# Another order of stages on four engines of a whole-program kernel

## What is computed

```python
# layer 0
mem = memory @ W_mem.T
attn = softmax(x @ mem.T / sqrt(D)); context = attn @ mem
gate = sigmoid(concat([x, context]) @ W_gate.T + b_gate)
x = rmsnorm(x + gate * context, norm_w)
# layers 1 and 3; vm: token and its successor are both of type 1
n = rmsnorm(x, ln_in); q, k, v = split(where(vm, n @ v_qkv, n @ l_qkv))      # 16 heads of 16
ctx = causal_attention(rotary(q), rotary(k), v)
x = x + where(vm, ctx @ v_dense, ctx @ l_dense)
x = x + cross_attention(rmsnorm(x, ln_cross) @ cq_w, context_rows @ ckv_w) @ cdense_w
m = rmsnorm(x, ln_post)
x = x + where(vm, mlp(m, v_weights), mlp(m, l_weights))      # down(silu(gate(m)) * up(m)), 688 wide
# layer 2
x = x + tanh(g1) * masked_attention(layernorm(x) @ Wq, media @ Wkv) @ Wo      # 16 heads of 64
x = x + tanh(g2) * gelu(layernorm(x) @ W1) @ W2
```

## Time and profile before

| | |
|---|---|
| median of 3 runs | 1376.25 us (1374.81 to 1379.65) |
| the profiled execution | 1375.08 us, its span 1372.8 us |
| mean granted TensorE clock of the span | 0.978 of full speed |
| TensorE busy | 1306.5 us (95%), 10931 matmuls |
| vector engine, ScalarE, GpSimd busy | 761.5, 467.8 and 457.3 us (55%, 34%, 33%) |
| DMA traffic | 27.28 MB, mean 20 GB/s |

### The profile page before, as it was taken

One profiled execution on the slowest core, in us unless ns is written; L12 is line 12 of the kernel. 1 busy time (PEld: TensorE's weight loads), 2 busy tenths in 40 slices (PEclk: granted clock), 3 DMA queues, 4 the chain that ended last, 5 costly groups with the idle time before them and its releaser, 6 DMA issues.

```text
span 1372.8 us, 25897 instructions
## 1 busy us (share of the span) xinstructions
PE 1306.5 (95%) x10931; PEld 1055.0 (77%) x10931; DVE 761.5 (55%) x1361; ACT 467.8 (34%) x779; POOL 457.3 (33%) x559
## 2 busy tenths in 40 slices
PE   7898899999999999999999999998899999999988
PEld 5775677877877778888888888876578777787766
DVE  2645666656656756444344553345566657576553
ACT  3333234324233133243344434433442332423321
POOL 1232444435434433311111211224444254344332
PEclk9787899999999999999999999999999999999999
DMA  9001000000001001120000000011000000000000
GB/s 321 12 2 61 2 2 2 1 2 2 1 2 47 1 5 43 44 72 1 0 1 1 1 0 1 1 42 42 1 2 1 2 17 1 2 17 2 1 16 16
DMA packets 19900, 27.28 MB, mean 20 GB/s; under 512 B 3432, under 2 KB 15552, under 8 KB 19520
## 3 DMA queue, kind: packets, MB, share of 16 engines
q1 hardware_dynamic: 19008, 24.20, 5.3%
q10 hardware_dynamic: 768, 1.26, 0.3%
HBM read 23.35 MB, written 2.10 MB: 19 GB/s over the span
## 4 chain that ended last, share of the span: by engine, by line
PE 81%; DVE 6%; POOL 5%; ACT 4%; issue 3%; ACTq 0%; DVEq 0%; POOLq 0%
PE bank L956 5%; PE bank L1100 5%; PE bank L1246 5%; PE bank L1211 4%; PE row_banks L1360 4%; PE bank L1216 4%; PE bank L1420 4%; PE bank L1463 4%; PE bank L1456 4%; PE row_banks L1083 4%; PE row_banks L1050 3%; PE bank L1235 3%; PE bank L949 2%; PE bank L1018 2%; PE bank L1221 2%
## 5 line engine op out<-in xcount | busy, mean ns | idle before, releaser
L1816 DVE TENSOR_REDUCE room<-row_banks 128x4 f32<-128x512 f32 (+1 forms) x128 | 116.5, 952 | 24.8 <-PE row_banks L1055 24.4
L806 POOL TENSOR_SCALAR_AFFINE_SELECT room<-room 128x1024 f32<-128x1024 f32 x64 | 70.4, 1103 | 167.6 <-ACT room L1574 167.6
L1574 ACT ACTIVATE room<-row_banks 128x1536 f32<-128x1536 f32 x64 | 93.0, 1452 | 81.7 <-PE row_banks L1083 81.6
L1246 PE MATMUL bank<-room,down_w 128*128 128x256 f32 x384 | 94.0, 384 | 0.5 <-DVE room L1916 0.5
L1606 ACT ACTIVATE room<-bank 128x256 f32<-128x256 f32 x96 | 36.4, 383 | 134.9 <-PE bank L1216 125.6
L1246 PEld LDWEIGHTS bank<-room,down_w 128*128 128x128 f32 x384 | 69.6, 190 | 12.3 <-issue 3.3
L1830 DVE RECIPROCAL room<-bank 128x256 f32<-128x256 f32 x32 | 56.1, 1754 | 39.3 <-PE bank L1100 39.2
L768 POOL TENSOR_TENSOR room<-room 128x256 f32<-128x256 f32 x32 | 24.7, 772 | 157.7 <-ACT room L1586 157.7
L1586 ACT ACTIVATE room<-x_all 128x512 f32<-128x512 f32 x32 | 20.2, 630 | 151.9 <-DVE x_all L1885 93.8
L1083 PE MATMUL row_banks<-room 32*128 32x256 f32 (+1 forms) x1024 | 62.8, 360 | 7.8 <-ACT room L1574 4.0
L1899 DVE SCALAR_TENSOR_TENSOR room<-room,bank 128x256 f32<-128x256 f32 x96 | 39.9, 416 | 53.3 <-ACT room L1606 53.2
(11 more groups left out here) (243 smaller groups left out, 3043.4 us busy)
## 6 DMA issues: line engine op xcount, KB each, us to landing
out_x<-wq SPq DMA_DIRECT2D x8, 256.0 KB, 2.3
qkv<-in_L_xattn_v_qkv SPq DMA_DIRECT2D x2, 768.0 KB, 5.9
qkv<-in_L_xattn_l_qkv SPq DMA_DIRECT2D x2, 768.0 KB, 8.9
gate_w<-in_L_xattn_v_gate SPq DMA_DIRECT2D x2, 640.0 KB, 8.6
gate_w<-in_L_xattn_l_gate SPq DMA_DIRECT2D x2, 640.0 KB, 7.5
up_w<-in_L_xattn_v_up SPq DMA_DIRECT2D x2, 640.0 KB, 6.0
...
```

What stands on the lines that cost most here:

```text
L806: pool.affine_select(out=diagonal, in_=diagonal, compare_op=ALU.is_ge, fill=0.0, base=0, pattern=[[0, 8], [1, P]], channel_multiplier=-1)\
L1246: return pe.matmul(ff_bank[0][:, t * S:(t + 1) * S], down_w[:, f, t * P:(t + 1) * P], hid[:, i, :], start=(i == t == 0), stop=(i == UPS - ...
L1574: act.activation(probs[w % 2], row_banks[:, :, 0:3 * P], ACT.Exp).then_inc(*ATT_ACT.does(e, f"exp{w}"))
L1816: last = dve.tensor_reduce(dst, row_banks[:, :, P * i:P + S * i], X, ALU.max, negate=True)
```

## The change

Only the table `ORDER` is written anew. It has the same stages for each engine, each once. Of TensorE's 1150 stages 496 stand at another place, of ScalarE's 613 345, of the vector engine's 723 358, of GpSimd's 401 239, of SyncE's 8 none; none is more than 13 places away from where it was. The table takes one line more, so each line number after it is one higher than before. The diff of the table, cut to a line of TensorE's old and new order and one of the vector engine's:

```diff
...
-        f_context.2 f_context.0 f_gate.2 f_gate.1 f_turn.3 f_context.3 f_sum.2 f_gate.0 f_spread.2 f_gate.3 f_sum.1
...
+        f_context.1 f_turn.3 f_gate.2 f_context.3 f_gate.1 f_gate.0 f_gate.3 f_sum.1 f_sum.2 f_sum.0 f_mem.0.3
...
-        f_gated.1 f_mean.2 p_seen.0 f_gated.0 f_mean.1 f_gated.3 f_mean.0 f_y.1 f_y.0 f_mean.3 f_y.2 f_shift.4
...
+        f_shift.0 p_one_hot.0 f_shift.2 f_shift.1 f_sums.0 p_trig_out.0 f_sums.2 f_sums.1 f_shift.3 f_sums.3 p_seen.0
...
```

More of the change, by code:

```diff
@@ L191 @@
-        first_scores.3.1 crs_spread.1.1 k.4 v.4 memory.2 first_scores.3.2 dense.2 up.1.0 up.1.1 crs_sum.2.0
-        first_scores.3.3 crs_spread.2.0 up.1.2 cross_q.2 n0_sum.5 up.1.3 n0_spread.5 cross_first.2 up.1.4 turn_max.3
-        up.1.5 second_scores.3.0 late_up.1.0 second_scores.3.1 values.3.0 cross_turn_max.2 second_scores.3.2
-        late_up.1.2 values.3.1 second_scores.3.3 late_up.1.1 cross_second.2 values.3.2 values.3.3 cross_values.2
-        down.1.0 late_down.1.0 late_down.1.1 late_down.1.2 cross_project.2 down.1.1 down.1.2 down.1.3 crs_sum.2.1
@@ L196 @@
-        down.1.4 down.1.5 crs_spread.2.1 first_scores.4.0 q.5 k.5 first_scores.4.1 memory.3 v.5 dense.3
+        first_scores.3.0 down.0.0 down.0.1 cross_project.1 down.0.2 down.0.3 down.0.4 crs_sum.1.1 first_scores.3.1
+        crs_spread.1.1 down.0.5 q.4 k.4 memory.2 first_scores.3.2 dense.2 v.4 up.1.1 up.1.0 crs_sum.2.0
+        first_scores.3.3 crs_spread.2.0 up.1.2 n0_sum.5 cross_q.2 up.1.3 n0_spread.5 cross_first.2 up.1.4 turn_max.3
+        up.1.5 second_scores.3.0 cross_turn_max.2 late_up.1.0 second_scores.3.1 values.3.0 late_up.1.2
@@ L202 @@
[L202 to L205 removed]
+        crs_spread.3.1 down.2.5 q.6 k.6 v.6 memory.4 first_scores.5.2 dense.4 up.3.0 up.3.1 crs_sum.4.0
@@ new lines @@
+        n0_spread.13 up.9.3 cross_first.10 up.9.4 turn_max.11 up.9.5 second_scores.11.0 late_up.9.0 second_scores.11.1
+        values.11.0 late_up.9.2 second_scores.11.2 cross_turn_max.10 values.11.1 second_scores.11.3 late_up.9.1
+        cross_second.10 values.11.2 values.11.3 cross_values.10 down.9.0 down.9.1 down.9.2 cross_project.10
+        late_down.9.0 down.9.3 down.9.4 down.9.5 crs_sum.10.1 late_down.9.1 late_down.9.2 crs_spread.10.1 turn_out.8
+        turn_out.9 first_scores.12.0 q.13 memory.11 first_scores.12.1 k.13 v.13 dense.11 first_scores.12.2 up.10.0
@@ L288 @@
[L288 to L291 removed]
+        cross_values.11 first_scores.13.0 down.10.0 down.10.1 cross_project.11 q.14 crs_sum.11.1 down.10.2 down.10.3
@@ new lines @@
+        crs_spread.11.1 down.10.4 down.10.5 v.14 memory.12 first_scores.13.1 k.14 up.11.0 dense.12 first_scores.13.2
+        n0_sum.15 up.11.1 crs_sum.12.0 up.11.2 crs_spread.12.0 n0_spread.15 first_scores.13.3 cross_q.12 up.11.3
+        cross_first.12 turn_max.13 up.11.4 up.11.5 second_scores.13.0 late_up.11.0 second_scores.13.1
+        cross_turn_max.12 values.13.0 second_scores.13.2 values.13.1 second_scores.13.3 late_up.11.1 cross_second.12
+        values.13.2 values.13.3 cross_values.12 down.11.0 down.11.1 late_up.11.2 down.11.2 down.11.3 down.11.4
```

561 lines of the change are left out of this document (276 added, 285 removed).

## The result

| | before | the new order |
|---|---|---|
| median, first comparison | 1377.53 us (4 runs, 1374.81 to 1379.65) | 1361.42 us (4 runs, 1354.47 to 1363.33) |
| ratio, 95% interval | | 0.9875 [0.9835, 0.9915] |
| the same kernel again, 5 runs | 1379.26 us (15 runs) | 1361.43 us, ratio 0.9873 [0.9854, 0.9893] |
| profiled execution, its span, clock | 1375.08, 1372.8 us, 0.978 | 1361.10, 1359.1 us, 0.979 |

The new order is 16 to 18 us faster, where 5 were forecast and 1363 was the lower end of the range. In the two profiles the difference is 14.0 us. Before's profiled execution was one of its quicker ones: of 62 runs of it beside the experiments nearly all took 1375 to 1381 us.

A forecast was written before the change was run, and what follows sets the result against it. TensorE's own work was taken as the bound (81% of the chain), so only waits and low clock could be won. Terms -3 - 0.5 + 0 - 0.5 - 0.7 + 0.5 + 0 = -4.2, with clock -5: 1371.2 us, range 1363 to 1380.

The forecast's parts named there:

- Fusion: Layer 0, 20 to 57 us: p_seen moves into the vector engine's 9.02 us hole, TensorE waits shrink; -3 us, bounds -2 and -4.5.
- what is late next is the first pow, which takes 3.02 us: Layer 0: GpSimd's first pow would end at 49.8 us, leaving TensorE a wait of 2.4 us ahead of f_spread.1.
- The three steady stretches: 200 to 560, 560 to 880 and 1020 to 1300 us: no wait worth filling, some stages late; +0.5 us, bounds 0 and +3.
- Hand-over: Layer 2 to 3, 880 to 900 us: n0_sum.9 and n0_spread.9 move into gaps of the chain; -0.5 us, bounds 0 and -0.9.
- Cross attention: 950 to 1000 us: v.11, values.9.3 and crs_sum.8.0 fill TensorE's waits; -0.7 us, bounds -1.5 and +1.5.
- 60 to 100 us: f_sum.7 moves behind f_spread.5, whose wait of 0.73 us shrinks as its mean comes earlier; -0.5 us, bounds 0 and -0.7.
- 100 to 200: 100 to 200 us, first expert: TensorE's order and its waits along the score chain stay; 0 us, bounds -0.6 and +0.6.
- The fall at 95.2 us: Low clock behind the 0.73 us wait, where 12 matmuls take 4.44 instead of 2.84 us; half of 1.6 us counted, 0.8.
- signs of being wrong: Include: steady stretches lack 3 us more or clock under 0.99; low time from 40 to 200 us over 10 off 48; f_gated.2 late.
- The clock: Whole kernel: with fewer waits some low clock goes, 0.8 us, taking the forecast from -4.2 to -5 us.
- The rival of more gain: Layer 0: the clock's fall at 54.2 us doesn't come, so 7.7 us more go; 1360 to 1366 us, chance 0.14.
- The slower rival: Steady stretches: new 1 us waits, each with a clock fall, cost 4.3 us apiece; 1380 to 1384 us, chance 0.18.

The follow-up runs named there:

- e2: The kernel before with only p_seen moved ahead of f_gated.2 on the vector engine; median 1375.58 us, ratio 0.9982.
- e5: The new kernel with p_seen moved back from ahead of f_gated.2 to behind f_mean.2, beside the pows; median 1368.13 us, ratio 0.9929 to the kernel before.
- e7: The kernel before with one GpSimd pair swapped, crs_rstd.3.0 ahead of turn_q.5; run once, 1380.44 us, only its timeline used.
- e11: The kernel before with the new order only from 888 to 1020 us of the old times; median 1376.14 us, ratio 0.9977.
- e10: The new kernel with the old order put back from 955 to 1020 us; median 1361.26 us, ratio 0.9873 to the kernel before.
- e4: The kernel before with the new order only from 880 to 1020 us of the old times; median 1380.31 us, ratio 1.0014.

## Why the prediction was wrong

**Sign and main mechanism were right**, and the size was wrong by a factor of three, outside the range. By its own steps:

- *Fusion, -3 us.* Measured -6.5 to -6.8 (6.0 from the start of the execution, where this one loaded 0.7 us late). p_seen went into the hole as said. The step that failed is "what is late next is the first pow, which takes 3.02 us": it was priced as a property of the first pow, and carried into the new order at full price, while it was p_seen that made it slow (e2, e5). That is 2.0 of the 3.6 us (a wait of 0.43 for one of 2.4). The rest is ahead of the gates: f_gate.2 starts at 29.64 us instead of 30.96, 14.1 instead of 16.1 us after x_turn.1, which I had set equal. The bound of -4.5 was too tight for the same reason.
- *The three steady stretches, +0.5 us with bounds 0 and +3.* Measured -4.7 up to 803 us and -0.8 from 1018 to 1306. This is the largest miss in sign. Two things failed: "there is no wait worth filling" was read from a busy share, which shows less than a wait costs (0.70 us for 0.48 shown), and the bounds left out any gain, though 8.5 us of idle time stood in the rows. The two table loads of ScalarE cost nothing that I can see, and no wait of TensorE there is longer than 0.61 us.
- *Hand-over, -0.5.* Measured -1.7: 0.2 to 0.4 by the moved work, no more than chance, and the rest by 3.4 us less at the low clock behind the wait, which I hadn't priced there and which isn't the order's (e7, e11).
- *Cross attention, -0.7.* The waits shrank by more than I said, the time didn't (+1.2 in the profile). Against e10, which has the old order there, it is -0.8, about as forecast. What hid it is the clock, 10 us more of it low than in before's profile.
- *60 to 100 us, -0.5 and 0.8 for the clock.* Measured -1.3 in all, which looks right, but by luck: the second profile of the same kernel has +0.4, with 14 us of low clock instead of 10. *100 to 200, 0:* -0.9. The fall at 95.2 us, which I had half going, is gone in both profiles of the new kernel, and v.0 runs at the high clock: that is 3.4 us less of low clock behind the start of v.0, and near the 0.8 that I had counted for it. From 40 to 200 us TensorE is low for 37 us in the new profile and 41 in the second, instead of 48; a difference over 10 was one of my signs of being wrong.
- *The clock.* Its part is 3 us smaller in the new kernel, where I had 0.8. The rival of more gain rested on the fall at 54.2 us not coming. It came, at 52.6 (49.5 in the second profile), and was shorter (10 and 14 instead of 17 us). The rival had the right size, 1360 to 1366, by luck: its mechanism gave 2 to 3 of its 8 us.
- *What it was measured against.* The profiled run and the median of three, 1376.25, were both on the quick side of before: its later medians are 1378.0 to 1379.3. That is 1 to 3 us of the miss.

The slower rival's price for one such place was near in sum (4.3 us forecast, 3.8 in e4) but not in its parts: 2.23 us of waiting instead of 1, and 1.6 of clock instead of 3.3. The new order makes no such wait.
